# One-hots laid out with the token column innermost, and unread products through the router's search

## The reference

```
capacity = ceil(T / E * 1.25)
logits = tokens @ router_w.T;  probs = softmax(logits)
top1_idx = argmax(probs);      top1_prob = max(probs)
order = lexsort((-top1_prob, top1_idx))
keep = position inside the expert's group < capacity
final_e = where(keep, top1_idx, 0)
for e in range(E):
    y = relu(tokens @ W1[e] + b1[e]) @ W2[e] + b2[e]
    out += where(final_e == e, y, 0)
```

## Time and profile before

| | us |
|---|---|
| median of 3 runs | 553.0 |
| lowest, highest | 550.98, 557.37 |
| the profiled execution | 551.12 |
| its span | 549.3 |

### The profile page before, as it was taken

The page is one execution under the profiler, slowest core; times in us unless marked ns, Lnnn a source line. Parts: engine busy times, 40 slices in busy tenths (PEclk is TensorE's granted clock), DMA queues, the critical chain, the costliest instruction groups (busy, mean ns, idle before and its releaser), DMA issues.

```text
span 549.3 us, 10418 instructions
## 1 busy us (share of the span) xinstructions
PE 385.4 (70%) x2861; PEld 306.3 (56%) x2861; DVE 377.2 (69%) x941; ACT 355.8 (65%) x827; POOL 198.3 (36%) x276
## 2 busy tenths in 40 slices
PE   0370427999999789768784232154999988898994
PEld 0230015699989633335552222053999877787894
DVE  2999997578888779949998887893454443343452
ACT  1589987678888469769973541052877656566572
POOL 7300192253535200000000000006667777777764
PEclk9999999999999989978997555576999999999998
DMA  9920000000000000000339900005656555555550
GB/s 214 251 62 1 1 0 0 2 1 2 0 0 0 1 1 1 0 0 2 79 79 252 236 12 1 0 1 191 211 210 219 199 175 179 174 190 185 187 196 30
DMA packets 45137, 48.67 MB, mean 89 GB/s; under 512 B 10232, under 2 KB 32800, under 8 KB 45088
## 3 DMA queue, kind: packets, MB, share of 16 engines
q1 hardware_dynamic: 39728, 38.59, 23.4%
q0 software_dynamic: 4096, 8.46, 5.8%
q10 hardware_dynamic: 1264, 1.03, 0.7%
HBM read 16.20 MB, written 8.45 MB: 45 GB/s over the span
## 4 chain that ended last, share of the span: by engine, by line
PE 30%; DVE 24%; ACT 15%; issue 14%; POOL 13%; DMA 3%; SPq 0%; POOLq 0%; DVEq 0%; ACTq 0%
POOL out L594 9%; PE psum L956 6%; PE psum L972 5%; DVE big L1546 4%; POOL xall L587 4%; PE psum L1138 3%; ACT xqT L759 2%; PE psum L964 2%; PE psum L1147 2%; ACT tok_b L759 2%; DMA keys<-in_ctx 2%; ACT big L662 2%; DVE xqT L1628 2%; DVE part L1322 2%; ACT big L619 1%
## 5 line engine op out<-in xcount | busy, mean ns | idle before, releaser
L587 POOL DMA_INDIRECT xall<-token_rows,src_of x64 | 62.0, 968 | 201.2 <-DVE slot_of L1675 182.0
L828 ACT ACTIVATE xqT<-psum,feat 128x128 f32<-128x128 f32 x284 | 81.0, 368 | 39.2 <-PE psum L1138 38.2
L1147 PE MATMUL psum<-keys,xqT 128*128 x568 | 78.3, 281 | 1.5 <-issue 1.1
L1138 PE MATMUL psum<-xqT,feat 128*128 128x128 f32 x568 | 77.1, 280 | 0.0
L594 POOL DMA_INDIRECT out<-xall,src_of x64 | 63.2, 987 | 27.6 <-issue 16.8
L1147 PEld LDWEIGHTS psum<-keys,xqT 128*128 128x128 f32 x568 | 68.8, 192 | 5.6 <-issue 4.6
L1138 PEld LDWEIGHTS psum<-xqT,feat 128*128 128x128 f32 x568 | 70.8, 196 | 0.0
L1697 DVE TENSOR_SCALAR xqT<-xall 128x128 f32 x71 | 26.0, 366 | 41.2 <-DMA xall<-token_rows,src_of 39.7
L1703 DVE TENSOR_TENSOR xqT<-psum,feat 128x128 f32<-128x128 f32 x71 | 20.7, 292 | 44.2 <-PE psum L1147 35.4
L561 POOL TENSOR_TENSOR qb<-qb,arec 128x308 f32<-128x308 f32 x32 | 21.8, 699 | 64.6 <-DVE arec L1380 64.6
L972 PE MATMUL psum<-probT,keys 78*128 78x128 f32 x256 | 34.8, 282 | 1.8 <-ACT probT L724 1.8
(11 more groups left out here) (301 smaller groups left out, 927.9 us busy)
## 6 DMA issues: line engine op xcount, KB each, us to landing
feat<-keys SPq DMA_DIRECT2D x71, 322.0 KB
token_rows<-xall SPq DMA_DIRECT2D x4, 1040.0 KB, 8.0
xall<-in_x SPq DMA_DIRECT2D x8, 512.0 KB, 7.1
keys<-in_L_ffn_W SPq DMA_DIRECT2D x1, 2048.0 KB, 13.1
keys<-in_L_ffn_W SPq DMA_DIRECT2D x8, 256.0 KB, 6.6
keys<-in_ctx SPq DMA_DIRECT2D x4, 462.0 KB, 6.8
xall<-token_rows,src_of POOLq DMA_INDIRECT x64
out<-xall,src_of POOLq DMA_INDIRECT x64, 2.6
```

The lines of the kernel that those rows point to most:

```text
L587: pool.indirect_dma_start(xring[:, t % RING, :], None, rows, bass.IndirectOffsetOnAxis(ap=src_of[:, t:t + 1], axis=0)).then_inc(s_g[t % TU ...
L828: m = act.activation(hT[a % DEPTH][:, P * c:P * c + P], bank(2 + a % 2)[:, P * c:P * c + P], ACT.Relu, bias=w_now[a % AHEAD][:, FF + c:FF ...
L1138: m = pe.matmul(bank(2 + a % 2)[:, P * c:P * c + P], w_now[a % AHEAD][:, P * c:P * c + P], gT[a % DEPTH], start=True, stop=True)
L1147: m = pe.matmul(bank(4 + a % 2, E), hT[a % DEPTH][:, P * c:P * c + P], w2s[:, bass.ds(e, 1), c, :].rearrange("p e d -> p (e d)"), start=(c ...
```

## The change

The one-hots get the token column innermost: `hot` and `hot_row` are now, for each block, arrays of (tile, column) and (row, column) with 16 adjacent columns. All operands are bf16: the compared numbers `tile_b` and `row_b` are written as bf16, and the constants `tile_no_b` and `row_no_b` are written out 16-fold by larger iotas at the start. VectorE also writes `hot_t`, `hot` times the column's number, with a wait for its own `hot`. ScalarE makes `hot_tile` in token order out of `hot` and `hot_t`, in two operations a block that read with a step of 16 elements. TensorE needs one product for each column, L1115 and its four accumulations go, and its stationary operand is read with a step of 16 elements. VectorE puts the result together in two operations instead of five. Apart from this, `keep_busy` is called through search and masks, into PSUM bank 7.

```diff
-        tile_no_b = sb("tile_no_b", [P, TILES], BF16)
-        row_no_b = sb("row_no_b", [P, P], BF16)
+        tile_no_b = sb("tile_no_b", [P, TILES, HT], BF16)
+        row_no_b = sb("row_no_b", [P, P, HT], BF16)
+        column_no_b = sb("column_no_b", [P, B], BF16)
+        tile_b = sb("tile_b", [P, B], BF16)
+        row_b = sb("row_b", [P, B], BF16)
...
-        hot_row = xqT[:, :].rearrange("p (t r) -> p t r", t=B)
-        hot_tile = feat[:, :].bitcast(BF16)[:, 0:B * 2 * TILES].rearrange("p (t a c) -> p t a c", t=B, a=2)
-        hot = qb[:, 0:B * TILES].rearrange("p (t c) -> p t c", t=B)
+        blocks = range(B // HT)
+        hot_row = [xqT[:, i * HT * P:(i + 1) * HT * P].rearrange("p (r t) -> p r t", t=HT) for i in blocks]
+        hot_tile = [feat[:, :].bitcast(BF16)[:, i * HT * 2 * TILES:(i + 1) * HT * 2 * TILES]
+                    .rearrange("p (t a c) -> p t a c", a=2, t=HT) for i in blocks]
+        hot_t = [tok_b[:, T // 2 + i * HT * TILES:T // 2 + (i + 1) * HT * TILES].rearrange("p (c t) -> p c t", t=HT)
+                 for i in blocks]
+        hot = [qb[:, i * HT * TILES:(i + 1) * HT * TILES].rearrange("p (c t) -> p c t", t=HT) for i in blocks]
...
             for i in range(B // HT):
-                act.wait_ge(s_ht, i + 1)
-                act.activation(hot_tile[:, i * HT:(i + 1) * HT, 0, :], hot[:, i * HT:(i + 1) * HT, :], ACT.Copy,
-                               scale=part_no[:, :])
-                for q in range(i * HT, (i + 1) * HT, QUARTER):
-                    m = act.activation(hot_tile[:, q:q + QUARTER, 1, :], hot[:, q:q + QUARTER, :], ACT.Copy,
-                                       scale=float(q // QUARTER))
-                m.then_inc(s_hp, 1)
+                act.wait_ge(s_ht, 2 * i + 1)
+                act.activation(hot_tile[i][:, :, 0, :], hot[i].rearrange("p c t -> p t c"), ACT.Copy, scale=part_no[:, :])
+                act.wait_ge(s_ht, 2 * i + 2)
+                act.copy(hot_tile[i][:, :, 1, :], hot_t[i].rearrange("p c t -> p t c")).then_inc(s_hp, 1)
...
+            keep_busy(16, bank(7))
             pe.wait_ge(s_v, 1)
...
             for k in range(LEVELS):
                 count_up(k, WAYS - 1)
+                keep_busy(6, bank(7))
             count_up(LEVELS, 4)
...
+            keep_busy(6, bank(7))
             ties, final = tok_b[:, 0:512], tok_b[:, 512:1024]
...
             pe.matmul(bank(6), not_before_b[:, :], ties, start=True, stop=True).then_inc(s_ps, 1)
+            keep_busy(12, bank(7))
             pe.wait_ge(s_ms, 2)
...
-                for t in range(i * HT, (i + 1) * HT):
-                    pe.matmul(bank(2, 2 * TILES), hot_row[:, t, :], hot_tile[:, t, :, :].rearrange("p a c -> p (a c)"),
-                              start=t == 0, stop=t == B - 1)
-                    n = t % QUARTER
-                    m = pe.matmul(psum[:, 3, n * TILES:(n + 1) * TILES], hot_row[:, t, :], hot[:, t, :],
-                                  start=t == 0, stop=t == B - 1)
+                for n in range(HT):
+                    m = pe.matmul(bank(2, 2 * TILES), hot_row[i][:, :, n], hot_tile[i][:, n].rearrange("p a c -> p (a c)"),
+                                  start=i + n == 0, stop=i * HT + n == B - 1)
...
             def one_hots(i):
-                t = slice(i * HT, (i + 1) * HT)
-                dve.tensor_tensor(hot[:, t, :], tile_no_b[:, :].unsqueeze(1).to_broadcast([P, HT, TILES]),
-                                  t64[4][:, t].unsqueeze(2).to_broadcast([P, HT, TILES]), ALU.is_equal
-                                  ).then_inc(s_ht, 1)
-                dve.tensor_tensor(hot_row[:, t, :], row_no_b[:, :].unsqueeze(1).to_broadcast([P, HT, P]),
-                                  t64[5][:, t].unsqueeze(2).to_broadcast([P, HT, P]), ALU.is_equal).then_inc(s_hr, 1)
+                def by_column(ap, n):
+                    return ap[:, i * HT:(i + 1) * HT].unsqueeze(1).to_broadcast([P, n, HT])
+                dve.tensor_tensor(hot[i], tile_no_b[:, :, :], by_column(tile_b, TILES), ALU.is_equal).then_inc(s_ht, 1)
+                dve.wait_ge(s_ht, 2 * i + 1)
+                dve.tensor_tensor(hot_t[i], hot[i], by_column(column_no_b, TILES), ALU.mult).then_inc(s_ht, 1)
+                dve.tensor_tensor(hot_row[i], row_no_b[:, :, :], by_column(row_b, P), ALU.is_equal).then_inc(s_hr, 1)
...
-            w = [big[:, (14 + j) * 512:(14 + j) * 512 + TILES] for j in range(2)]
-            rest = [psum[:, 3, n * TILES:(n + 1) * TILES] for n in range(QUARTER)]
-            ch.link(dve.tensor_copy(w[0], rest[1]))
-            ch.join()
-            do(dve.scalar_tensor_tensor(w[0], rest[2], 2.0, w[0], ALU.mult, ALU.add))
-            do(dve.scalar_tensor_tensor(w[0], rest[3], 3.0, w[0], ALU.mult, ALU.add))
-            do(dve.scalar_tensor_tensor(w[1], bank(2)[:, TILES:2 * TILES], float(QUARTER), w[0], ALU.mult, ALU.add))
-            dve.scalar_tensor_tensor(src_of[:, :], w[1], float(P), bank(2)[:, 0:TILES], ALU.mult, ALU.add
-                                     ).then_inc(s_idx, 1)
+            w = big[:, 14 * 512:14 * 512 + TILES]
+            do(dve.tensor_copy(w, bank(2)[:, 0:TILES]))
+            dve.scalar_tensor_tensor(src_of[:, :], bank(2)[:, TILES:2 * TILES], float(P), w, ALU.mult, ALU.add
+                                     ).then_inc(s_idx, 1)
```

More of the change, by code:

```diff
@@ L41 @@
 LAG = 17
-QUARTER = 4
 HS = G // 2
@@ L261, in xattn_moe @@
         t64 = [sb(f"t64_{n}", [P, B]) for n in range(6)]
-        t64i = [sb(f"t64i_{n}", [P, B], I32) for n in range(3)]
-        hot_row = xqT[:, :].rearrange("p (t r) -> p t r", t=B)
-        hot_tile = feat[:, :].bitcast(BF16)[:, 0:B * 2 * TILES].rearrange("p (t a c) -> p t a c", t=B, a=2)
-        hot = qb[:, 0:B * TILES].rearrange("p (t c) -> p t c", t=B)
+        blocks = range(B // HT)
[5 more added lines that the diff above has]
+        hot = [qb[:, i * HT * TILES:(i + 1) * HT * TILES].rearrange("p (c t) -> p c t", t=HT) for i in blocks]
         s_ctx = [sem(f"ctx_loaded{n}") for n in range(NP)]
@@ L533, in _ @@
             pool.memset(spans[:, 1, 0:1], 0.0).then_inc(s_const, 1)
-            pool.iota(tile_no_b[:, :], pattern=[[1, TILES]], base=0, channel_multiplier=0,
+            pool.iota(tile_no_b[:, :, :], pattern=[[1, TILES], [0, HT]], base=0, channel_multiplier=0,
                       allow_small_or_imprecise_dtypes=True).then_inc(s_const, 1)
-            pool.iota(row_no_b[:, :], pattern=[[1, P]], base=0, channel_multiplier=0,
+            pool.iota(row_no_b[:, :, :], pattern=[[1, P], [0, HT]], base=0, channel_multiplier=0,
+                      allow_small_or_imprecise_dtypes=True).then_inc(s_const, 1)
+            pool.iota(column_no_b[:, :], pattern=[[1, B]], base=0, channel_multiplier=0,
                       allow_small_or_imprecise_dtypes=True).then_inc(s_const, 1)
@@ L1619, in _ @@
             do(dve.tensor_scalar(t64[2][:, :], position, 0.5 - P / 2, 1.0 / P, ALU.add, ALU.mult))
-            do(dve.tensor_scalar(t64[4][:, :], t64[2][:, :], MAGIC, MAGIC, ALU.add, ALU.subtract))
-            do(dve.scalar_tensor_tensor(t64[5][:, :], t64[4][:, :], -float(P), position, ALU.mult, ALU.add))
+            do(dve.tensor_scalar(tile_b[:, :], t64[2][:, :], MAGIC, MAGIC, ALU.add, ALU.subtract))
+            do(dve.scalar_tensor_tensor(row_b[:, :], tile_b[:, :], -float(P), position, ALU.mult, ALU.add))
             def one_hots(i):
-                t = slice(i * HT, (i + 1) * HT)
-                dve.tensor_tensor(hot[:, t, :], tile_no_b[:, :].unsqueeze(1).to_broadcast([P, HT, TILES]),
-                                  t64[4][:, t].unsqueeze(2).to_broadcast([P, HT, TILES]), ALU.is_equal
-                                  ).then_inc(s_ht, 1)
-                dve.tensor_tensor(hot_row[:, t, :], row_no_b[:, :].unsqueeze(1).to_broadcast([P, HT, P]),
-                                  t64[5][:, t].unsqueeze(2).to_broadcast([P, HT, P]), ALU.is_equal).then_inc(s_hr, 1)
+                def by_column(ap, n):
[4 more added lines that the diff above has]
+                dve.tensor_tensor(hot_row[i], row_no_b[:, :, :], by_column(row_b, P), ALU.is_equal).then_inc(s_hr, 1)
             for i in range(B // HT):
```

## The result

The changed kernel takes 556.45 us (median of 7 runs, 555.34 to 558.86); the kernel before took 553.0 in 7 runs on the same chip. The ratio is 1.0066, 95% interval 1.0041 to 1.0091: slower by 3.65 us (the medians lie 3.45 apart), small but outside what is noise between the two. The prediction, 547.2 with a range up to 553.5, is wrong in sign, and the time lies above its range.

What follows compares the result with a forecast made beforehand. The prediction took the serial chain ahead of GpSimd's first gather as the bound, moving the tail 1:1. Gains 1.5 + 0.8 + 2.5 = 4.8 us gave 546.3 from the profiled execution, 548.2 from the median; forecast 547.2, range 543.0 to 553.5.

Steps and rivals of the forecast that it cites:

- Parts 1 to 3: One-hots to first read of the products: 15.3 us after the first one-hot starts instead of 16.8, gain 1.5 us.
- Part 1: VectorE's one-hots in 16-bit, token innermost: 2.47 us a block, four blocks 9.9 instead of 13.35 us, gain 3.5.
- part 2: ScalarE's two stepped-read operations a block: 1.81 and 1.70 us, 3.3 a block after overlap, so ScalarE bounds the stage.
- Stepped reads set the time, not an addition: Rival: ScalarE pays 1.68 ns per element, 2.0 and 1.9 us an operation, 3.7 a block; total 547.8 us; chance 0.14.
- part 3: TensorE's placing products, one per column: hidden under ScalarE's 3.3 us a block except 1.3 us for the last block.
- Part 4: Fewer VectorE steps from the products to the first gather: 0.76 us instead of 1.54, gain 0.8.
- Part 5: Unread TensorE products in search and masks keep the clock up: no delay, gain 2.5 us, two thirds of 3.7.
- The rival for slower: ScalarE's bf16 stepped reads: slower from 4.5 us a block; at 3.4 ns extra per element, 569 us; chance 0.06.

Runs made afterwards that it cites:

- e3: The kernel before plus two unread wide iotas (1024 and 2048 elements) at the change's place, nothing else: 555.92 us, ratio 1.0061.
- e10: The changed kernel with only the two wide iotas moved, from the start to when VectorE begins to read the logits: 553.43 us, ratio 1.0009.
- e5: e4 plus unread ScalarE copies at different steps, and unread TensorE products with one operand stepped in place of 12 fillers: one run, 554.44 us.
- e2: The changed kernel without the `keep_busy` calls: 557.01 us, ratio 1.0078.
- e1: The kernel before plus only the `keep_busy` calls (unread products): 549.75 us, ratio 0.9944.
- e4: The changed kernel with small iotas, which ScalarE writes out 16-fold while idle ahead of the one-hots: 553.86 us, ratio 1.0016.
- e11: e4 without its fillers (the unread products): 554.99 us, ratio 1.0021.
- e7: e6 plus the change's unread products: 546.22 us, ratio 0.9877.
- e6: The kernel before with only the row one-hot in the new layout, its wide numbers written by ScalarE in the mask stage: 549.15 us, ratio 0.9922.

## Why the prediction was wrong

**The step that failed** is "The larger iotas run on GpSimd at the very start, and nothing reads them before the one-hots: 0". It asked only who reads the tiles. They cost 3.3 us of the critical path: e3 adds them alone (+3.4), e10 moves them (1.0009 against 1.0066, -3.2). In the trace of before the quantising step already lay beside a small iota, at 18.87; the question "what does VectorE do while GpSimd works longer?" wasn't asked. This step is what made the kernel slower. It isn't the whole miss: with the iotas moved (e10) the kernel is as fast as before, and the forecast 4.8 us are still missing, through the parts below.

**Parts 1 to 3** were to bring 1.5 us and cost 2.5: the first read of the products came 19.36 us after the first one-hot (357.32 to 376.68) instead of the forecast 15.3. Part 1 was right to the hundredth: 0.69, 0.69, 1.22, 2.47 us a block, 9.87 for four. In part 2 the mechanism was right, ScalarE bounds the stage, but the term was mis-sized: 4.14 us a block instead of 3.3, together 3.4 us. The value came from a VectorE row whose extra 0.64 ns per element was added to ScalarE's own time; e5 has 0.96 ns per element for ScalarE. The rival "Stepped reads set the time, not an addition" was nearer with 2.0 and 1.9 us for an operation; measured were 2.15 to 2.35 and 2.01 to 2.04. Its total, 547.8, missed for the other reasons; like those of the other rivals it was counted from the profiled execution, 551.12, and the forecast from 552.0, so the two don't compare as they stand. In part 3 the stationary step is nearly free, as hoped, but the last 16 products took 1.90 instead of 1.3 us: between the blocks TensorE now pauses 2.2 us and its granted clock is 0.50 from 357 to 372, where the earlier trace rows had 0.97 in 363 to 372.

**Part 4** was right: 0.78 us from the read to the gather (376.68 to 377.46), forecast 0.76.

**Part 5** was to bring 2.5 us; in the profile of after it brought 1.42. The warm price of a pair, 0.39, and a warm level, 3.81, are near what was worked out, but the transposes of the keys were cold all the same (1.97 us), and of the levels only those behind some 322 us were warm. The table has 1.4 us for the fillers in after against e2, 1.8 in e1, 1.8 in e4 against e11 and 2.6 in e7 against e6; the transposes took 1.97 in the first three and 1.09 in e7. So the gain follows how much of the stretch ran warm. In the medians the fillers are worth 3.0 us in the kernel before (e1), 2.9 from e6 to e7, but 0.6 from e2 to the changed kernel and about 1.1 from e11 to e4. Intervals of 0.2 to 0.3% on each ratio (1 to 2 us) don't exclude one common value near 2.

**The sum.** In the span: +3.3 for the iotas instead of 0, +2.5 instead of -1.5 for parts 1 to 3, -0.8 for part 4, -1.4 instead of -2.5 for part 5, and +0.9 and +0.5 in stages that the change doesn't touch: +5.0. The 0.9 can't be laid on the change: from the first scale step to the first read of the logits before takes 273.64 us (19.64 to 293.28) and after 274.56, but e6, which leaves that stretch alone, takes 274.75 (19.73 to 294.48), and e10, which has the change's layout, 273.45 (20.33 to 293.78).

The rival for slower looked for the loss at ScalarE's bf16 steps, from 4.5 us a block on. ScalarE stayed below that (4.14). No rival had a mechanism outside the stages that the change rewrites, and the chance given to slower by over 1% was 0.08. The result, 0.7% slower, lies in the part within 1% that had 0.54, but not by the terms of the sum.

## What to carry to other kernels

A constant that is made larger isn't free because nobody reads it soon: look at what runs beside it on the engine that shares its ports, above all a one-input VectorE operation on the critical path beside GpSimd, and move it under other work. A layout that doubles VectorE's speed has to be priced at each reader too: keep the distance of a reader's steps at 8 bytes, which cost next to nothing here, and put longer steps on the stationary operand. A term taken over from another engine's row needs both forms as bounds, extra time on top of the reader's own and a time that replaces it.

## What had not been expected of the hardware

- ScalarE's stepped reads are a stair: 1.04, 1.04, 1.10, 2.02, 2.04 us for 1024 bf16 elements at steps of 2, 4, 8, 16 and 32 bytes, and float32 has the stair at the same bytes. The Trainium skill, "SBUF — State Buffer", on SBUF's two sides, asks for two hits on a 16-byte line, and that is where the stair stands. The same note lets one stride 4 float32 or 8 bf16 elements for free; both are 16 bytes, and here they cost 0.48 and 0.98 us more.
- With a step of 32 bytes a moving operand makes a product of 128 columns over 4 times as long (0.24 against 0.055 us), a stationary one adds 0.01 us.
- A waiting VectorE operation was passed over, in after and again in e3: the second iota started at 19.95 (20.27 in e3), more than 1 us after it, and still ran first.
- In e7 TensorE was busy for 13.49 of the 15 us from 304 to 319 at a granted clock of 0.50 (1.2 GHz), and for 7.68 of the 15 us from 321 to 336 at 1.00 (2.4 GHz). Heavy DMA alone isn't what withholds the clock, since 296 to 302 had 1.00 with more traffic (323 against 215 GB/s); what decides the moment when it rises stays open.

```profile
296.00:302.00 6.00, 2.97 (x18) 1.00 1.04 323
304.00:319.00 15.00, 13.49 (x37) 0.50 1.10 215
321.00:336.00 15.00, 7.68 (x39) 1.00 0.00 1
```
